# Layer norms ahead of the experts and the relative attention: the reciprocal root by a power on GpSimd, and all their coefficients made there

## The chip, the cores and the metric

The kernel runs on one NeuronCore of a Trainium2 chip. The metric is the device time of one execution in microseconds (us), lower is better. The engines are TensorE (PE; its weight loads are PEld), VectorE (DVE), ScalarE (ACT), GpSimd (POOL) and SyncE (SP, which issues DMAs). Each runs its own instruction stream, and they meet at semaphores.

## The reference

The reference is a sequence of four transformer-like layers on x of shape (8, 512, 128) in float32. Each layer is `x = x + attention(_layernorm(x))` and then `x = x + experts(_layernorm(x))`. All norms are

```python
def _layernorm(x, axis=-1, eps=1e-05):
    m = jnp.mean(x, axis=axis, keepdims=True)
    v = jnp.var(x, axis=axis, keepdims=True)
    return (x - m) / jnp.sqrt(v + eps)
```

The change concerns five of the eight norms: those ahead of the four expert blocks (top-2 GLU experts L0, switch experts L1, expert choice L2, threshold experts L3) and the one ahead of the relative-position attention of layer 3. The expert blocks also need `xn @ router` (8 or 9 columns) and a softmax over it.

## The kernel before

x stays in on-chip memory for the whole program, as 32 tiles of 128 tokens x 128 features (`chip.x`); a sequence is `TPS` = 4 tiles, and there are `B` = 8 sequences. The eight blocks run one after another. Each stage is an `nc.Block()` that gives every engine its own program and ends in a barrier over all engines.

`normalise_and_route` is one such stage and is called five times: as l0f, l1f, l2f and l3f (names of tiles carry this prefix) ahead of the experts, with a router, and as l3a ahead of the relative attention, with no router. It loops over the 8 sequences, fully unrolled, in this order for sequence i:

- VectorE makes the statistics of four tiles (`bn_stats` L513, then `bn_aggr` L517), which gives mean and variance in `mv`, 128x4 of each.
- ScalarE makes `std` = sqrt(variance + eps) (L545).
- VectorE makes `rstd` (reciprocal, L527) and `shift` = -mean x rstd (L528).
- GpSimd makes the normalised rows `xn_all` = x * rstd + shift, one instruction for a tile (L537).
- TensorE transposes the four tiles into one PSUM bank (L575), ScalarE copies the bank out (L557), and with a router TensorE multiplies the copy by it (L564), one sequence behind the transposes.
- In l0f and l1f SP stores the rows of a sequence to memory (L499) as soon as they are made.

`stats`, `mv`, `std`, `rstd` and `shift` are double-buffered. VectorE works one sequence ahead: statistics(i+1) stand before the reciprocal of sequence i. ScalarE too has the root of i+1 ahead of the copy of i. After the stage comes `route`, where VectorE takes the logits from PSUM, subtracts their maximum (L641), and ScalarE takes Exp (L715). ScalarE's functions come from tables; a function that isn't in the set loaded last has an ACT_TABLE_LOAD ahead of it, under its own line.

Two helpers matter. `Chain.link(ins)` makes an instruction count a semaphore and lets its engine wait for it, so that the next instruction starts when this one is complete. `chip.apart(eng)` puts one instruction on the engine that only counts a semaphore.

Of the kernel before, what the change touches and what calls it, by code (L numbers as in the profile page):

```python
# [7 lines left out]
ALU = mybir.AluOpType  # L8
ACT = mybir.ActivationFunctionType
# [5 lines left out]
P = 128  # L15
D = 128
B, S = 8, 512
TPS = S // P
NT = B * TPS
U = 2  # L20
LN_EPS = 1e-5
# [77 lines left out]
class Chip:  # L99


    def __init__(self, nc, ctx):
        self.nc, self.ctx = nc, ctx
        self.x = self.sb(ctx, "x", [P, NT, D])
        self.ident = self.sb(ctx, "ident", [P, P])
        self.ones = self.sb(ctx, "ones", [P, P])
        self.ln_eps = self.sb(ctx, "ln_eps", [P, 1])
        self.before = self.sb(ctx, "before", [P, P])
        self.count = self.sb(ctx, "count", [P, P])
        self.by_distance = nc.dram_tensor("by_distance", (H3, SPAN + 1), F32, kind="Internal").ap()  # L110
        self.by_place = nc.dram_tensor("by_place", (H3, P, SPAN + 1), F32, kind="Internal").ap()
        self.biases_placed = nc.alloc_semaphore(name="biases_placed")
        self.zeros = self.sb(ctx, "zeros", [P, D])
        self.token_no = self.sb(ctx, "token_no", [P, NUMBERS])
        self.apart_count = nc.alloc_semaphore(name="apart_count")
        self.counts = []
        self.banks = ctx.enter_context(nc.psum_tensor("bank", [P, 8, BANK], F32))
        self.psum = [self.banks[:, k, :] for k in range(8)]
# [9 lines left out]
    def sem(self, name):  # L128
        self.counts.append(self.nc.alloc_semaphore(name=name))
        return self.counts[-1]  # L130
# [29 lines left out]
def load_stage(chip, x_in, ident_in, before_in, count_in, token_in, rel_bias, onehot_in):  # L160


    nc = chip.nc
    inner = ExitStack()
    table, onehot, line = (chip.sb(inner, n, shape) for n, shape in (("table", [BUCKETS, H3]), ("onehot", [BUCKETS, SPAN + 1]),
                                                                      ("line", [H3, SPAN + 1])))
    table_loaded, summed, lined, line_stored = (chip.sem(n) for n in ("table_loaded", "summed", "lined", "line_stored"))
    loaded = chip.sem("x_loaded")
    with inner, nc.Block() as block:
        @block.sync  # L170
        def _(sp):
            sp.dma_start(chip.ident[:], ident_in).then_inc(loaded, 16)
            xv = x_in.rearrange("b (t p) d -> p (b t) d", p=P)
            for c in range(2):
                h = NT // 2
                sp.dma_start(chip.x[:, c * h:(c + 1) * h, :], xv[:, c * h:(c + 1) * h, :]).then_inc(loaded, 16)
            sp.dma_start(chip.before[:], before_in).then_inc(loaded, 16)
            sp.dma_start(chip.count[:], count_in.partition_broadcast(P)).then_inc(loaded, 16)
            sp.dma_start(chip.token_no[:], token_in).then_inc(loaded, 16)
            sp.wait_ge(loaded, 96)  # L180

        @block.vector
        def _(dve):
            nc.vector.memset(chip.ones[:], 1.0)
            nc.vector.memset(chip.ln_eps[:], LN_EPS)
            nc.vector.memset(chip.zeros[:], 0.0)
            for c in range(2):
                dve.wait_ge(summed, c + 1)
                dve.tensor_scalar(line[:, c * S:(c + 1) * S], chip.psum[c][0:H3, :], -1.0, None, ALU.mult).then_inc(lined, 1)

        @block.scalar
        def _(act):
            act.dma_start(table[:], rel_bias).then_inc(table_loaded, 16)
            act.dma_start(onehot[:], onehot_in).then_inc(table_loaded, 16)
            act.wait_ge(lined, 2)
            act.dma_start(chip.by_distance, line[:]).then_inc(line_stored, 16)
            act.wait_ge(line_stored, 16)

        @block.tensor
        def _(pe):  # L200
            pe.wait_ge(table_loaded, 32)
            for c in range(2):
                pe.matmul(chip.psum[c][0:H3, :], table[:], onehot[:, c * S:(c + 1) * S], start=True, stop=True).then_inc(summed, 1)
# [265 lines left out]
def normalise_and_route(chip, ctx, L, w_router, turned_out=True, rows_out=None, load_behind=None):  # L469
# [3 lines left out]
    nc = chip.nc  # L473
# [3 lines left out]
    with ExitStack() as inner:  # L477
        sb = lambda name, shape: chip.sb(inner, f"{L}r_{name}", shape)
        two = lambda name, shape: [sb(f"{name}{u}", shape) for u in range(2)]
        sem = lambda name: chip.sem(f"{L}r_{name}")  # L480
        router = sb("router", [P, NR]) if NR else None
        stats, mv = two("stats", [P, TPS, 6]), two("mv", [P, TPS, 2])
        std, rstd, shift = two("std", [P, TPS]), two("rstd", [P, TPS]), two("shift", [P, TPS])
        xnT = [xnT_all[:, i * S:(i + 1) * S] for i in range(B)] if turned_out else two("xnT", [P, S]) * (B // 2)
        loaded, stored = sem("loaded"), sem("rows_stored")
        mv_ready, std_ready, shift_ready, xn_ready = sem("mv_ready"), sem("std_ready"), sem("shift_ready"), sem("xn_ready")
        turned, xnT_ready, routed = sem("turned"), sem("xnT_ready"), sem("routed")
        dve_order = sem("dve_order")
        with nc.Block() as block:
            @block.sync  # L490
            def _(sp):
                if NR:
                    sp.dma_start(router[:], w_router).then_inc(loaded, 16)
                if rows_out is not None:
                    sp.dma_start(rows_out[0:1, :], chip.zeros[0:1, 0:D]).then_inc(stored, 16)
                    for i in range(B):
                        sp.wait_ge(xn_ready, i + 1)
                        rows = rows_out[1 + i * S:1 + (i + 1) * S, :].rearrange("(t p) d -> p t d", p=P)
                        sp.dma_start(rows, xn_all[:, i * TPS:(i + 1) * TPS, :]).then_inc(stored, 16)  # L499
                if load_behind:  # L500
                    if NR:
                        sp.wait_ge(loaded, 16)
                    load_behind(sp)
                if rows_out is not None:
                    sp.wait_ge(stored, 16 * (B + 1))

            @block.vector
            def _(dve):
                c = Chain(dve, dve_order)

                def statistics(i):
                    for t in range(TPS):
                        ins = dve.bn_stats(stats[i % 2][:, t, :], chip.x[:, i * TPS + t, :])  # L513
                    c.link(ins)
                    chip.apart(dve)
                    for t in range(TPS):
                        ins = dve.bn_aggr(mv[i % 2][:, t, :], stats[i % 2][:, t, :])  # L517
                    ins.then_inc(mv_ready, 1)

                statistics(0)  # L520
                for i in range(B):
                    if i + 1 < B:
                        statistics(i + 1)
                    dve.wait_ge(std_ready, i + 1)
                    if i >= 2:
                        dve.wait_ge(xn_ready, i - 1)
                    c.link(dve.reciprocal(rstd[i % 2][:], std[i % 2][:]))  # L527
                    dve.scalar_tensor_tensor(shift[i % 2][:], mv[i % 2][:, :, 0], -1.0, rstd[i % 2][:], ALU.mult,  # L528
                                             ALU.mult).then_inc(shift_ready, 1)

            @block.gpsimd
            def _(pool):
                for i in range(B):
                    pool.wait_ge(shift_ready, i + 1)
                    chip.apart(pool)
                    for t in range(TPS):
                        ins = pool.tensor_scalar(xn_all[:, i * TPS + t, :], chip.x[:, i * TPS + t, :], rstd[i % 2][:, t:t + 1],  # L537
                                                 shift[i % 2][:, t:t + 1], ALU.mult, ALU.add)
                    ins.then_inc(xn_ready, 1)

            @block.scalar
            def _(act):
                def deviation(i):
                    act.wait_ge(mv_ready, i + 1)
                    act.activation(std[i % 2][:], mv[i % 2][:, :, 1], ACT.Sqrt, bias=chip.ln_eps[:]).then_inc(std_ready, 1)  # L545

                deviation(0)
                for i in range(B):
                    if i + 1 < B:
                        deviation(i + 1)  # L550
                    if not (turned_out or NR):
                        continue
                    act.wait_ge(turned, i + 1)
                    if not turned_out and i >= 2:
                        act.wait_ge(routed, i - 1)
                        chip.apart(act)
                    act.copy(xnT[i][:], chip.psum[4 + i % 4][:]).then_inc(xnT_ready, 1)  # L557
# [1978 lines left out]
```

## Time and profile before

| | us |
|---|---|
| median of 3 runs | 3579.72 (3578.07 to 3584.71) |
| profiled execution, its own time | 3584.16 |
| span of that execution, first to last instruction | 3582.4 |
| TensorE matmul busy | 2932.5 |
| VectorE busy | 1922.8 |
| ScalarE busy | 1517.0 |
| GpSimd busy | 1198.6 |

The profile is of one execution. Busy times of engines overlap, so they don't add up to the span. A stretch of the program between two barriers lasts as long as its slowest chain, whatever the busy shares over the whole are.

### The profile page before, as it was taken

How to read it: one execution, taken by the hardware profiler on the slowest of the kernel's cores; microseconds unless marked ns; L12 is line 12 of the kernel's file. 1: busy time of each engine (PE TensorE's matmuls, PEld its weight loads, DVE VectorE, ACT ScalarE, POOL GpSimd, SP SyncE). 2: the span in 40 equal slices, each digit the busy share in tenths (PEclk: the TensorE clock that was granted, in tenths of full speed). 3: DMA queues.
4: the chain of work that ended last, by engine and by line, in shares of the span. 5: the costliest groups of instructions: out<-in, count | busy, mean ns of one | idle time of the engine just before them, and what ended most of it. 6: DMA issues, size and time to landing. Idle time of an engine off the chain costs nothing. (4 is left out here: it accounts for less than half of the span.)

```text
span 3582.4 us, 49632 instructions
## 1 busy us (share of the span) xinstructions
PE 2932.5 (82%) x15224; PEld 1877.2 (52%) x15224; DVE 1922.8 (54%) x4857; ACT 1517.0 (42%) x3087; POOL 1198.6 (33%) x1106
## 2 busy tenths in 40 slices
PE   7868985866845665666589599999999999799998
PEld 4658974656711221224589444444444444577776
DVE  4444446544178997997644355555555555311111
ACT  3322323121335445543233256665665666244443
POOL 0014761113715650664000245555555555200000
PEclk9977997656967996998799799999999999799999
DMA  4004661002510000001000200000000000000000
GB/s 134 0 24 135 208 174 39 0 3 86 161 34 1 1 1 0 0 0 47 1 0 0 106 1 1 0 0 0 0 0 0 0 0 1 13 6 12 6 12 23
DMA packets 75742, 110.37 MB, mean 31 GB/s; under 512 B 13442, under 2 KB 46228, under 8 KB 75588
## 3 DMA queue, kind: packets, MB, share of 16 engines
q1 hardware_dynamic: 67268, 91.70, 8.1%
q0 software_dynamic: 8192, 16.79, 2.1%
q8 instruction: 51, 0.84, 0.1%
q14 instruction: 103, 0.84, 0.1%
q10 hardware_dynamic: 128, 0.20, 0.0%
HBM read 93.91 MB, written 23.14 MB: 33 GB/s over the span
## 5 line engine op out<-in xcount | busy, mean ns | idle before, releaser
L1496 POOL TENSOR_TENSOR l3a_p<-l3a_p,l3a_rden 128x512 f32<-128x512 f32 x512 | 520.9, 1040 | 487.0 <-DVE l3a_rden L1535 484.6
L1525 DVE CUSTOM_DVE_ANT_0 l3a_p<-bank,l3a_bias 128x512 f32<-128x512 f32 x512 | 333.2, 688 | 201.5 <-PE bank L1674 195.4
L2211 POOL TENSOR_TENSOR l2a_dBu<-l2a_work,l2a_bs 128x1024 f32<-128x1024 f32 x128 | 303.3, 2373 | 327.3 <-ACT l2a_bs L2276 327.3
L1595 ACT ACTIVATE l3a_p<-l3a_p,l3a_low 128x512 f32<-128x512 f32 x512 | 365.4, 718 | 7.5 <-DVE l3a_low L1525 7.0
L1683 PEld LDWEIGHTS bank<-ident,l3a_p 128*128 128x128 f32 x2048 | 228.3, 140 | 166.8 <-issue 158.0
L2357 DVE TENSOR_TENSOR_SCAN l2a_h<-bank,l2a_dBu 128x1024 f32<-128x1024 f32 x128 | 291.9, 2281 | 5.2 <-POOL l2a_dBu L2211 5.2
L1674 PE MATMUL bank<-l3a_kT,l3a_qT 64*128 64x512 f32 x1024 | 291.2, 645 | 1.1 <-ACT l3a_kT L1586 0.7
L1601 ACT COPY l3a_pT<-bank 128x512 f32<-128x512 f32 x256 | 150.3, 587 | 324.8 <-PE bank L1683 324.4
L844 DVE SCALAR_TENSOR_TENSOR x<-bank,l3f_gates,x 128x128 f32 x256 | 85.5, 351 | 371.7 <-PE bank L872 371.7
L1683 PE MATMUL bank<-ident,l3a_p 128*128 128x128 f32 x2048 | 274.9, 277 | 3.3 <-DVE l3a_pT L1531 2.7
L2407 PE MATMUL bank<-l2a_bc,l2a_pick 128*128 128x512 bf16 x256 | 99.8, 399 | 183.4 <-DVE l2a_hc L2389 141.6
L2457 PE MATMUL bank<-l2a_hc,ident 128*128 128x512 f32 x512 | 246.5, 605 | 2.2 <-DVE l2a_xc L2363 2.2
L872 PEld LDWEIGHTS bank<-l3fe_w,l3fe_h 128*128 128x128 f32 x2048 | 233.7, 192 | 15.3 <-issue 15.3
L1692 PE MATMUL bank<-l3a_pT,l3a_v 128*64 128x512 f32 x1024 | 233.8, 598 | 0.0
L872 PE MATMUL bank<-l3fe_w,l3fe_h 128*128 128x128 f32 x2048 | 233.8, 275 | 0.0
L864 PE MATMUL bank<-l3f_xnT_all,l3fe_w 128*128 x512 | 227.3, 597 | 5.5 <-DMA l3fe_w<-in_L_ffn_W_dram 5.5
L821 ACT ACTIVATE l3fe_h<-bank,l3f_b 128x512 f32<-128x512 f32 x256 | 168.4, 689 | 142.8 <-PE bank L864 139.7
L1531 DVE COPY l3a_pT<-bank 128x512 f32<-128x512 f32 x256 | 174.4, 681 | 67.3 <-PE bank L1683 53.0
L2407 PEld LDWEIGHTS bank<-l2a_bc,l2a_pick 128*128 128x128 bf16 x256 | 25.0, 98 | 303.5 <-DVE l2a_hc L2389 225.5
L2284 ACT ACTIVATE bank<-l2a_dt,l2a_a_neg 128x511 f32<-128x511 f32 x256 | 167.0, 689 | 21.2 <-DVE l2a_h L2357 21.1
L2276 ACT COPY l2a_bs<-bank 128x512 f32<-128x512 f32 x128 | 74.9, 585 | 212.9 <-PE bank L2407 212.9
L1674 PEld LDWEIGHTS bank<-l3a_kT,l3a_qT 64*128 64x128 f32 x1024 | 78.5, 186 | 162.0 <-issue 157.2
(495 smaller groups left out, 5178.7 us busy)
## 6 DMA issues: line engine op xcount, KB each, us to landing
l0fe_wi<-in_L_ffn_in_dram SPq DMA_DIRECT2D x40, 516.0 KB, 4.7
l0fe_wo<-in_L_ffn_out_dram SPq DMA_DIRECT2D x40, 320.0 KB, 3.4
by_place<-by_distance SPq DMA_DIRECT2D x16, 512.0 KB, 11.6
l1fe_wo<-in_L_ffn_out_dram SPq DMA_DIRECT2D x24, 320.0 KB, 3.1
l3a_bias<-by_place SPq DMA_DIRECT2D x16, 448.0 KB, 12.3
l1fe_wi<-in_L_ffn_in_dram SPq DMA_DIRECT2D x24, 258.0 KB, 3.6
l0fe_answers<-l0f_y_rows SPq DMA_DIRECT2D x16, 256.0 KB, 5.0
l3fe_w<-in_L_ffn_W_dram SPq DMA_DIRECT2D x16, 256.0 KB, 3.0
```

Source lines behind the costliest of these rows:

```text
L864: bk.fill(pe.matmul(ps((n, u, j))[:], w[eh][:, j * P:(j + 1) * P], rhs, start=True, stop=True), (n, u, j))
L872: ins = pe.matmul(ps(("y", u))[:, t * D:(t + 1) * D], h[u][:, j, t * P:(t + 1) * P], w2s[eh][:, j, :], start=(j == 0), stop=(j == J - 1))
L1496: ins = pool.tensor_tensor(a, a, rden[:, t, h:h + 1].to_broadcast([P, S]), ALU.mult)
L1525: bk.drain(dve.tensor_tensor_reduce(p[u % 2][h][:, t, :], ps(job)[:], bias[:, u % HP * 2 + h, b0:b0 + S], 1.0, 3.0e38, ALU.add, ALU.min, l ...
L1531: bk.drain(dve.tensor_copy(pT[h][:, kt, :], ps(job)[:]), job)
L1595: ins = act.activation(a, a, ACT.Exp, bias=low[h][:, t:t + 1], scale=-1.0, accum_out=den[:, t, h:h + 1])
L1674: bk.fill(pe.matmul(ps(job)[:], qT[u % 2][half[h], t * P:(t + 1) * P], kT[u % 2][half[h], :], start=True, stop=True), job)
L1683: ins = pe.transpose(ps(job)[:, t * P:(t + 1) * P], p[u % 2][h][:, t, kt * P:(kt + 1) * P], chip.ident[:])
L1692: ins = pe.matmul(ps("av")[half[h], :], v[u // GP % 2][:, kt, c:c + DK3], pT[h][:, kt, :], start=(kt == 0), stop=(kt == TPS - 1))
L2211: dBu_ready.by(pool.tensor_tensor(dBu[q][:], work[u][:], bcast(bs[q][:], n_before=CH), ALU.mult))
L2357: h_ready.by(dve.tensor_tensor_scan(h[m % NH][:].rearrange("p c s -> p (c s)"), dA[m % NA].rearrange("p c s -> p (c s)"), dBu[q][:].rearra ...
L2457: ins = pe.matmul(ps(("y", u, j))[:], chip.ident[:], hc[m % NH][:, j, :], start=(n == 0), stop=(n == N - 1))
```

## The change

In `normalise_and_route` ScalarE no longer takes the root, and VectorE no longer makes reciprocal and shift; VectorE only makes the statistics. GpSimd waits for them, and makes with four instructions on 128x4: variance + eps, that to the power -0.5 (the exponent from a new constant tile `minus_half`), mean x rstd, and the product negated. Each is linked, and a counting instruction (`chip.apart`) stands ahead of each. Then come the four normalising instructions as before. Statistics of sequence i wait for the shift of sequence i-2.

```diff
--- before.py
+++ after.py
@@ -110,6 +110,7 @@
         self.by_distance = nc.dram_tensor("by_distance", (H3, SPAN + 1), F32, kind="Internal").ap()
         self.by_place = nc.dram_tensor("by_place", (H3, P, SPAN + 1), F32, kind="Internal").ap()
         self.biases_placed = nc.alloc_semaphore(name="biases_placed")
+        self.minus_half = self.sb(ctx, "minus_half", [P, 1])
         self.zeros = self.sb(ctx, "zeros", [P, D])
         self.token_no = self.sb(ctx, "token_no", [P, NUMBERS])
         self.apart_count = nc.alloc_semaphore(name="apart_count")
@@ -183,6 +184,7 @@
         def _(dve):
             nc.vector.memset(chip.ones[:], 1.0)
             nc.vector.memset(chip.ln_eps[:], LN_EPS)
+            nc.vector.memset(chip.minus_half[:], -0.5)
             nc.vector.memset(chip.zeros[:], 0.0)
             for c in range(2):
                 dve.wait_ge(summed, c + 1)
@@ -485,7 +487,7 @@
         loaded, stored = sem("loaded"), sem("rows_stored")
         mv_ready, std_ready, shift_ready, xn_ready = sem("mv_ready"), sem("std_ready"), sem("shift_ready"), sem("xn_ready")
         turned, xnT_ready, routed = sem("turned"), sem("xnT_ready"), sem("routed")
-        dve_order = sem("dve_order")
+        dve_order, pool_order = sem("dve_order"), sem("pool_order")
         with nc.Block() as block:
             @block.sync
             def _(sp):
@@ -517,22 +519,25 @@
                         ins = dve.bn_aggr(mv[i % 2][:, t, :], stats[i % 2][:, t, :])
                     ins.then_inc(mv_ready, 1)
 
-                statistics(0)
                 for i in range(B):
-                    if i + 1 < B:
-                        statistics(i + 1)
-                    dve.wait_ge(std_ready, i + 1)
                     if i >= 2:
-                        dve.wait_ge(xn_ready, i - 1)
-                    c.link(dve.reciprocal(rstd[i % 2][:], std[i % 2][:]))
-                    dve.scalar_tensor_tensor(shift[i % 2][:], mv[i % 2][:, :, 0], -1.0, rstd[i % 2][:], ALU.mult,
-                                             ALU.mult).then_inc(shift_ready, 1)
+                        dve.wait_ge(shift_ready, i - 1)
+                    statistics(i)
 
             @block.gpsimd
             def _(pool):
+                c = Chain(pool, pool_order)
                 for i in range(B):
-                    pool.wait_ge(shift_ready, i + 1)
+                    pool.wait_ge(mv_ready, i + 1)
                     chip.apart(pool)
+                    c.link(pool.tensor_scalar(std[i % 2][:], mv[i % 2][:, :, 1], LN_EPS, 0.0, ALU.add, ALU.add))
+                    chip.apart(pool)
+                    c.link(pool.tensor_tensor(rstd[i % 2][:], std[i % 2][:], chip.minus_half[:].to_broadcast([P, TPS]), ALU.pow))
+                    chip.apart(pool)
+                    c.link(pool.tensor_tensor(shift[i % 2][:], mv[i % 2][:, :, 0], rstd[i % 2][:], ALU.mult))
+                    chip.apart(pool)
+                    c.link(pool.tensor_scalar(shift[i % 2][:], shift[i % 2][:], -1.0, 0.0, ALU.mult, ALU.add))
+                    pool.sem_inc(shift_ready, 1)
                     for t in range(TPS):
                         ins = pool.tensor_scalar(xn_all[:, i * TPS + t, :], chip.x[:, i * TPS + t, :], rstd[i % 2][:, t:t + 1],
                                                  shift[i % 2][:, t:t + 1], ALU.mult, ALU.add)
@@ -540,14 +545,7 @@
 
             @block.scalar
             def _(act):
-                def deviation(i):
-                    act.wait_ge(mv_ready, i + 1)
-                    act.activation(std[i % 2][:], mv[i % 2][:, :, 1], ACT.Sqrt, bias=chip.ln_eps[:]).then_inc(std_ready, 1)
-
-                deviation(0)
                 for i in range(B):
-                    if i + 1 < B:
-                        deviation(i + 1)
                     if not (turned_out or NR):
                         continue
                     act.wait_ge(turned, i + 1)
```

GpSimd's stream at its first instructions in l0f, where `l0fr_` are the small tiles of this stage. Before:

```order
L531 UNCONDITIONAL_BRANCH
L537 ISA
L537 TENSOR_SCALAR l0f_xn_all<-x,l0fr_rstd,l0fr_shift 128x128 x32
L489 UNCONDITIONAL_BRANCH
L1039 UNCONDITIONAL_BRANCH
```

And of the change, the first two of the eight sequences (its lines stand two to four away from those of before):

```order
L527 UNCONDITIONAL_BRANCH
L533 ISA
L533 TENSOR_SCALAR l0fr_std<-l0fr_mv 128x4
L535 TENSOR_TENSOR l0fr_rstd<-l0fr_std,minus_half 128x4
L537 TENSOR_TENSOR l0fr_shift<-l0fr_mv,l0fr_rstd 128x4
L539 TENSOR_SCALAR l0fr_shift<-l0fr_shift 128x4
L542 TENSOR_SCALAR l0f_xn_all<-x,l0fr_rstd,l0fr_shift 128x128 x4
L533 TENSOR_SCALAR l0fr_std<-l0fr_mv 128x4
L535 TENSOR_TENSOR l0fr_rstd<-l0fr_std,minus_half 128x4
```

The 32 normalising instructions stood in one run, and now each four of them have four small ones ahead.

VectorE's stream at the same place, before:

```order
L513 BN_STATS l0fr_stats<-x 128x6 x4
L517 BN_AGGR l0fr_mv<-l0fr_stats 128x2 x4
L513 BN_STATS l0fr_stats<-x 128x6 x4
L517 BN_AGGR l0fr_mv<-l0fr_stats 128x2 x4
L527 RECIPROCAL l0fr_rstd<-l0fr_std 128x4
L528 SCALAR_TENSOR_TENSOR l0fr_shift<-l0fr_mv,l0fr_rstd 128x4
```

And of the change:

```order
L515 BN_STATS l0fr_stats<-x 128x6 x4
L519 BN_AGGR l0fr_mv<-l0fr_stats 128x2 x4
L515 BN_STATS l0fr_stats<-x 128x6 x4
L519 BN_AGGR l0fr_mv<-l0fr_stats 128x2 x4
L515 BN_STATS l0fr_stats<-x 128x6 x4
```

The reciprocal and the shift are gone from VectorE, here and for each further sequence. On ScalarE the 40 roots of the five stages are gone, and with them nine table loads in the compiled order: the five at L545 and the four at L715.

## Rows read from the trace of the kernel before

**Rows 1.** The page, part 1: busy us, share of the span, instructions.

```profile
PE 2932.5 (82%) x15224; PEld 1877.2 (52%) x15224; DVE 1922.8 (54%) x4857; ACT 1517.0 (42%) x3087; POOL 1198.6 (33%) x1106
```

**Rows 2.** Busy times by stretch, l0f and l3a: length, engines, granted clock, DMA.

```profile
214.00:240.60 26.60, 20.30 (x96) 19.74 (x96) 11.89 (x80) 7.71 (x17) 13.86 (x32) 0.54 0.29 80
2016.00:2037.50 21.50, 8.93 (x32) 5.73 (x32) 11.81 (x80) 7.74 (x17) 13.89 (x32) 0.50 0.57 221
```

**Rows 3.** Timeline, start of l0f: start, duration, engine, line, operation [idle before].

```profile
213.97 1.28 ACT L545 ACT_TABLE_LOAD   x1 [16.14 <-PEq L135]
214.01 0.87 DVE L513 BATCH_NORM_STATS2 l0fr_stats<-x 128x6 f32<-128x128 f32 x4 [1.08 <-PEq L135]
215.03 0.38 DVE L517 BATCH_NORM_AGGREGATE l0fr_mv<-l0fr_stats 128x2 f32<-128x6 f32 x4
...
216.60 0.14 DVE L527 RECIPROCAL l0fr_rstd<-l0fr_std 128x4 f32<-128x4 f32 x1
...
216.78 0.16 DVE L528 SCALAR_TENSOR_TENSOR l0fr_shift<-l0fr_mv,l0fr_rstd 128x4 f32<-128x4 f32 x1
...
217.23 3.45 POOL L537 TENSOR_SCALAR l0f_xn_all<-x,l0fr_rstd,l0fr_shift 128x128 f32<-128x128 f32 x8 [216.77 <-DVE l0fr_shift L528]
...
219.11 1.09 PE L575 MATMUL bank<-ident,l0f_xn_all 128*128 128x128 f32 x4 [7.71 <-POOL l0f_xn_all L537]
```

**Rows 4.** Timeline, end of l0f and start of its route stage.

```profile
230.98 1.74 POOL L537 TENSOR_SCALAR l0f_xn_all<-x,l0fr_rstd,l0fr_shift 128x128 f32<-128x128 f32 x4 [0.72 <-DVE l0fr_shift L528]
...
233.43 1.74 POOL L537 TENSOR_SCALAR l0f_xn_all<-x,l0fr_rstd,l0fr_shift 128x128 f32<-128x128 f32 x4 [0.72 <-DVE l0fr_shift L528]
...
235.71 1.09 PE L575 MATMUL bank<-ident,l0f_xn_all 128*128 128x128 f32 x4
...
240.67 1.28 ACT L715 ACT_TABLE_LOAD   x1 [3.14 <-PEq L489]
...
241.62 0.42 DVE L641 TENSOR_TENSOR l0fg_a<-l0fg_logits,l0fg_red 128x256 f32<-128x256 f32 x1
```

**Rows 5.** Timeline, start and end of l3a.

```profile
2016.21 1.28 ACT L545 ACT_TABLE_LOAD   x1 [17.23 <-PEq L1446]
2016.98 0.38 DVE L517 BATCH_NORM_AGGREGATE l3ar_mv<-l3ar_stats 128x2 f32<-128x6 f32 x4
...
2032.17 3.48 POOL L537 TENSOR_SCALAR l3a_xn_all<-x,l3ar_rstd,l3ar_shift 128x128 f32<-128x128 f32 x8 [0.89 <-DVE l3ar_shift L528]
```

**Rows 6.** Timeline, layer 1's attention: an engine ends and GpSimd starts.

```profile
568.84 0.75 DVE L1882 TENSOR_SCALAR l1a_q<-bank,l1a_bq 128x512 f32<-128x512 f32 x1 [5.76 <-PE bank L2019]
569.67 1.04 POOL L1970 TENSOR_TENSOR l1a_qsq<-l1a_q 128x512 f32<-128x512 f32 x1 [5.99 <-DVE l1a_q L1882]
...
584.30 1.06 ACT L1989 ACTIVATE l1a_fq<-l1a_fq 128x1024 f32<-128x1024 f32 x1 [14.62 <-DVEq L1916]
585.56 1.04 POOL L1975 TENSOR_SCALAR l1a_fq<-l1a_fq 128x1024 f32<-128x1024 f32 x1 [6.03 <-ACT l1a_fq L1989]
```

**Rows 7.** Groups of GpSimd instructions by shape: busy us, mean ns | idle before.

```profile
L1046 POOL DMA_INDIRECT l0fe_xs<-l0f_xn_rows,l0f_source x80 | 83.4, 1042 | 85.8 <-issue 84.9 <-DVE l0fe_y L1097 0.9
...
L1970 POOL TENSOR_TENSOR l1a_qsq<-l1a_q 128x512 f32<-128x512 f32 x8 | 8.3, 1040 | 83.8 <-DVE l1a_q L1882 83.8
...
L2202 POOL CAST l2a_pick<-l2a_part_of 128x4096 bf16<-128x4096 f32 x1 | 3.6, 3597 | 10.9 <-DMA l2a_d_par<-in_L_attn_D_param_dram 10.9
L1965 POOL TENSOR_TENSOR l1a_feat<-l1a_head_of,l1a_proj 128x256 f32<-128x256 f32 x1 | 0.6, 618 | 32.9 <-DMA l1a_bfc<-in_L_attn_bfc_dram 32.9
L1489 POOL COPY l3a_xT<-l3a_xnT_all 128x512 f32<-128x512 f32 x1 | 0.6, 609 | 2.1 <-POOLq L489 2.1
L2199 POOL MEMSET l2a_xi<- 128x6 f32 x4 | 0.2, 103 | 14.8 <-POOLq L135 14.8
```

**Rows 8.** Groups by line: the table loads of roots and of Exp.

```profile
L545 ACT ACT_TABLE_LOAD x5 | 6.4, 1283 | 65.5 <-PEq L135 48.2 <-PEq L1446 17.2
L715 ACT ACT_TABLE_LOAD x4 | 5.1, 1283 | 11.6 <-PEq L489 11.6
```

## The prediction

> **What bounds the kernel now.** I read the page first, for shares only: no engine fills the span, TensorE is busiest at 82% and GpSimd stands at 33% [rows 1]. That says nothing of this change, because the function it touches, `normalise_and_route`, is a stage of its own between barriers. So I took the five stretches in which it runs (l0f from 214.0, l1f from 799.3, l2f from 1668.7, l3a from 2016.0, l3f from 3064.7 us) and asked for each engine's busy time in them [rows 2]: two of the five stand there. Each of the four with a router lasts some 26 us and the l3a one 21.5, together 127 us, 3.6% of the span. In l0f TensorE is busy 20.3 of 26.6 us, GpSimd 13.9, VectorE 11.9, ScalarE 7.7. In l3a, which has no router matmuls, TensorE needs 8.9 and GpSimd is the busiest, 13.9 of 21.5.
>
> Then the timelines. At the start [rows 3] a sequence goes VectorE statistics, ScalarE root, VectorE reciprocal and shift, GpSimd's four normalising instructions, TensorE. The first aggregate ends at 215.41 (215.03 + 0.38), the first shift at 216.94, and GpSimd begins at 217.23. At the end [rows 4] the steady state is to be seen: GpSimd starts a sequence at 230.98 and the next at 233.43, a period of 2.45 us, of which it works 1.74 and waits 0.71. TensorE sets that period in the routed stages (1.09 for four transposes, the rest for the router). GpSimd thus has 0.71 us a sequence to give before it becomes the bound itself. In l3a [rows 5] the last GpSimd work ends at 2035.65 (2032.17 + 3.48); nothing but the chain of engines sets the pace there.
>
> **The change, part by part.** Taken away for each sequence: one ScalarE root, one VectorE reciprocal, one VectorE shift, and the two crossings between them. Added on GpSimd: add epsilon, power, product, negation, each 128x4, each linked (it waits for the one before to finish, and a count instruction stands between). Call the time from the start of the first of the four to the start of the first normalising instruction T4. GpSimd then works T4 + 1.74 for each of eight sequences. The statistics come early enough: they take 1.25 us of VectorE (0.87 and 0.38), which now does nothing else, and they may start when the shift two sequences back is done, so a whole GpSimd period lies ahead. Queued behind the four on GpSimd are the normalising instructions, and TensorE, ScalarE's copies and, in l0f and l1f, SP's row stores wait for those.
>
> A routed stage. First aggregate 215.41; GpSimd wakes 0.21 us after another engine's end when a count instruction stands ahead of its work, as 585.36 (584.30 + 1.06) to 585.56 shows for ScalarE to GpSimd, while without one it is 0.08 (569.59 to 569.67) [rows 6]. So it starts at 215.62 and ends its last sequence at 215.62 + 8 x (T4 + 1.74) = 229.54 + 8 T4. Before, that end was 235.17 (233.43 + 1.74) [rows 4]. Behind it TensorE took 0.54 us to start the last transposes since it was still routing; GpSimd-bound it starts after 0.14, as the first did (217.23 and half of the 3.45 is 218.97, to 219.11) [rows 3]: 0.40 less. The router's last matmuls stay. Change: 229.54 + 8 T4 - 235.17 - 0.40 = 8 T4 - 6.03.
>
> The l3a stage. First aggregate 2017.36, so 2017.57 + 13.92 + 8 T4 = 2031.49 + 8 T4 against 2035.65, and the tail is the same: 8 T4 - 4.16 [rows 5].
>
> All five: 4 x (8 T4 - 6.03) + 8 T4 - 4.16 = **40 T4 - 28.3**. Break-even is T4 = 0.71 us.
>
> T4 itself. Four gaps (three links and the one to the normalising) at 0.21 = 0.84; the lower bound is 0.08 each. Plain instructions [rows 7]: two-input 618 ns at 256 elements and 1040 at 512, so 1.65 ns an element and 196 ns fixed; one-input 609 ns at 512 and 3597 at 4096, so 0.83 ns and 182 fixed. At 4 elements: 0.20 for the product, 0.19 each for the add and the negation, together 0.58. Lower bound 0.10 each, a memset of 6 elements; upper bound 0.44, a quarter of the 1.74 group.
>
> The power is in no row. Below, it costs a plain two-input instruction, 0.20. Above, it must be a routine in software of many such steps on each element; twenty plain instructions would be 4.0. I take 1.0, five steps, and the nearest row with real work and little data: an indirect-DMA issue, 1.04 us [rows 7]. T4 = 0.84 + 0.58 + 1.0 = 2.42, and 40 x 2.42 - 28.3 = +68.5. The Trainium skill, "GPSIMD Engine Reference", section "Engine selection", says to keep elementwise work on VectorE, GpSimd being about half as fast at two-input work. The trace agrees in direction, since the shift that now takes two GpSimd instructions took VectorE 0.16 us [rows 3]; by a factor of two alone on VectorE's old reciprocal and shift (0.14 and 0.16) T4 would be 0.6, an estimate, and the sum -4, which lies with the second rival below.
>
> **Table loads.** The compiled order has nine fewer ScalarE table loads, five for the root and four for the Exp of `route`, 1.28 us each [rows 8]. I cost them at nothing. The root's load ran 213.97 to 215.25 while VectorE made the statistics until 215.41 [rows 3]; in l3a it ended 2017.49, 0.13 after the aggregate [rows 5], and my l3a term starts from the aggregate already. Exp's load ended 241.95, while its operand was ready at 242.04 (241.62 + 0.42) [rows 4]; the other stages with that load have the same or a later operand. If cover were missing, it would be 9 x 1.28 = 11.5 us. The Trainium skill, "ScalarE: Activation LUTs", section "Rules for kernel authors", would budget about 2.7 us for each switch of set, which is 24 us for nine, and speaks for the change; the trace has 1.28 for a load and shows it beside other work.
>
> TensorE's granted clock is 0.54 and 0.50 in these stretches [rows 2], so about its lower level of 1.2 GHz; longer pauses have little to take away, and I add nothing for it.
>
> The sum is made on the profiled execution, 3584.2 us outside and 3582.4 in the span, which is 4.4 above the median of 3579.7. The difference added to the median: 3579.7 + 68.5 = **3648**.
>
> **Rivals.**
> First, a power that goes by a long routine, or takes elements one by one. No row excludes it. Fifty plain steps are 10 us, T4 11.4, +428: 4008. Chance 0.12, for everything above T4 = 5.4.
> Second, no change: GpSimd's four pass cheaply in the 0.71 us that it waits now. It needs T4 under 0.89 (7.2 us, which is 0.2% and about what a measurement of this kernel tells). With gaps at 0.08 and instructions at 0.10 T4 is 0.32 + 0.30 + 0.20 = 0.82, +4.5: 3584. Against it: the 0.21 is seen with this very count instruction ahead. Chance 0.05.
> Third, faster: the table loads turn out to be on the path (-11.5) and T4 is small. It decides at T4 = (28.3 + 11.5 - 7.2) / 40 = 0.815. At 0.7 it gives 28 - 28.3 - 11.5 = -12: 3568. In the routed stages TensorE's 2.45 us floor stops any larger gain. Both conditions speak against their rows; chance 0.03.
> The forecast, slower by T4 between 1.34 and 5.4, has 0.80.
>
> **How the numbers follow.** Low end: gaps 0.84, three plain instructions at 0.10 and the power at 0.20, T4 1.34, +25: 3605. High end: power at 4.0, T4 = 5.42, +188.5: 3768. What lies outside is the first rival above and the other two below, 0.20. Slower 0.92, within 0.2% 0.05, faster 0.03.
>
> **What would show it.** In the profile after: GpSimd instructions of 128x4 with idle gaps near 0.21 between them; the power as the longest of the four; the last normalising group of l0f ending 8 x T4 + 14.1 us after the first aggregate; TensorE waiting for GpSimd at each sequence; no table load in these stages; the `route` stage unchanged in length. The prediction fails if the power is far from 1 us (every 0.1 is 4 us), if the links cost GpSimd much more or less than 0.21, or if something behind the stages becomes shorter with the loads gone.

## The result, and the profile after

The changed kernel takes 3650.5 us, the median of 4 runs (3646.7 to 3661.5), against 3578.9 for the kernel before in the same comparison. The ratio is 1.0207, with a 95% interval of 1.0176 to 1.0238: slower by 72 us. The prediction was 3648 in a range of 3605 to 3768. The profiled execution took 3649.3, with a span of 3647.6.

The page of the changed kernel, part 1, answers to [rows 1]. GpSimd has 67 us more and 160 more instructions, four in each of 40 sequences.

```profile
PE 2925.4 (80%) x15224; PEld 1872.7 (51%) x15224; DVE 1914.2 (52%) x4778; ACT 1494.5 (41%) x3038; POOL 1265.5 (35%) x1266
```

The busy times of l0f and l3a after the change answer to [rows 2]. Both stretches run from the first statistics to the next stage's first work. They are about 14 and 16 us longer, with GpSimd now the busiest in both, at 27.2.

```profile
212.40:253.10 40.70, 21.16 (x96) 20.13 (x96) 9.86 (x65) 4.68 (x8) 27.20 (x64) 0.52 0.18 52
2048.30:2086.00 37.70, 8.92 (x32) 5.72 (x32) 9.86 (x64) 4.68 (x8) 27.22 (x65) 0.50 0.30 122
```

The timeline at the start of l0f after the change answers to [rows 3].

```profile
213.38 0.38 DVE L519 BATCH_NORM_AGGREGATE l0fr_mv<-l0fr_stats 128x2 f32<-128x6 f32 x4
...
214.03 0.23 POOL L533 TENSOR_SCALAR l0fr_std<-l0fr_mv 128x4 f32<-128x4 f32 x1 [213.59 <-DVE l0fr_mv L519]
214.45 1.04 POOL L535 TENSOR_TENSOR l0fr_rstd<-l0fr_std,minus_half 128x4 f32<-128x4 f32 x1 [0.18 <-POOL l0fr_std L533]
...
215.67 0.20 POOL L537 TENSOR_TENSOR l0fr_shift<-l0fr_mv,l0fr_rstd 128x4 f32<-128x4 f32 x1 [0.18 <-POOL l0fr_rstd L535]
216.07 0.20 POOL L539 TENSOR_SCALAR l0fr_shift<-l0fr_shift 128x4 f32<-128x4 f32 x1 [0.20 <-POOL l0fr_shift L537]
...
216.48 1.74 POOL L542 TENSOR_SCALAR l0f_xn_all<-x,l0fr_rstd,l0fr_shift 128x128 f32<-128x128 f32 x4 [0.21 <-POOL l0fr_shift L539]
...
218.30 0.23 POOL L533 TENSOR_SCALAR l0fr_std<-l0fr_mv 128x4 f32<-128x4 f32 x1
```

T4, from the start of the add at 214.03 to the first normalising instruction at 216.48, is 2.45 us: 0.23, the power's 1.04, twice 0.20, and four gaps of 0.18, 0.18, 0.20 and 0.21. In the other sequences it is 2.43 or 2.44, except for a few pauses, the longest in l0f's fourth sequence (T4 2.80). After the group of 1.74 another 0.08 passes before the next add (218.22 to 218.30), so a sequence takes 4.26.

The end of l0f and the start of its route stage answer to [rows 4]. The last group ends at 248.38, TensorE has waited for it, and there is no table load ahead of Exp.

```profile
246.64 1.74 POOL L542 TENSOR_SCALAR l0f_xn_all<-x,l0fr_rstd,l0fr_shift 128x128 f32<-128x128 f32 x4 [0.21 <-POOL l0fr_shift L539]
...
248.44 1.11 PE L573 MATMUL bank<-ident,l0f_xn_all 128*128 128x128 f32 x4 [1.63 <-POOL l0f_xn_all L542]
...
254.46 0.42 ACT L713 ACTIVATE l0fg_ex<-l0fg_a 128x256 f32<-128x256 f32 x1 [4.18 <-DVE l0fg_a L639]
```

The whole program holds more than these stages, and its other stretches differ between executions. So I split every profiled span in two: the five stages, each from its first statistics to the first work of the next stage, and all the rest. The lengths are worked out from the first starts of the tiles concerned in the traces; each is rounded by itself, and a sum can differ from its rounded terms by 0.1. l1f and l3f end when a small DMA with the biases has landed, which VectorE waits for; in l3f that DMA took 0.6 us longer in the changed kernel, which is part of its 43.4.

| kernel | stages l0f, l1f, l2f, l3a, l3f | sum | all the rest |
|---|---|---|---|
| before | 26.7, 28.7, 26.3, 21.8, 28.7 | 132.2 | 3450.2 |
| changed | 40.7, 42.9, 40.3, 37.7, 43.4 | 205.1 | 3442.5 |

The stages account for +72.9 and the rest for -7.7, which makes the span's +65.2.

### The profile page after: what moved, and what is told of

It reads as the page before. It is cut to its first block and busy times, and to the rows that moved or that the text cites. A ratio compares the mean times of both kernels' runs of the same rounds, so it can differ in the third digit from the quotient of the medians.

```text
span 3647.6 us, 49794 instructions
## 1 busy us (share of the span) xinstructions
PE 2925.4 (80%) x15224; PEld 1872.7 (51%) x15224; DVE 1914.2 (52%) x4778; ACT 1494.5 (41%) x3038; POOL 1265.5 (35%) x1266
## 6 DMA issues: line engine op xcount, KB each, us to landing
l3a_bias<-by_place SPq DMA_DIRECT2D x16, 448.0 KB, 11.5
```

## The experiments

The first four ran beside 15 runs of the kernel before with a median of 3580.0, e5 to e8 beside 16 with 3581.3. Their stage sums can be set beside 132.2 and 205.1.

### e1_product: a product in place of the power

```diff
-c.link(pool.tensor_tensor(rstd[i % 2][:], std[i % 2][:], chip.minus_half[:].to_broadcast([P, TPS]), ALU.pow))
+c.link(pool.tensor_tensor(rstd[i % 2][:], std[i % 2][:], chip.minus_half[:].to_broadcast([P, TPS]), ALU.mult))
```

> The changed kernel with the power's operation replaced by a plain product of the same two tiles, so the root isn't computed and the rows are scaled wrongly. My theory: the power costs its profile duration on GpSimd's own chain, so each falls from 1.03 to about 0.20 us, T4 from 2.44 to 1.61 us, and the program by 40 x 0.83 = 33 us to about 3617. Rival (what costs is the number of linked instructions, and the power's long duration overlaps the crossings): less than 10 us, so 3640 or more.

Measured: 3625.7 (3621.0 to 3626.7), ratio 1.0120 (1.0105 to 1.0136); stages 34.0, 36.0, 33.6, 31.0, 36.7, sum 171.4. The group in l0f:

```profile
L535 POOL TENSOR_TENSOR l0fr_rstd<-l0fr_std,minus_half 128x4 f32<-128x4 f32 x8 | 1.6, 198 | 1.8 <-POOL l0fr_std L533 1.8
```

The stages fell by 33.7, where 33 was expected. The power is paid in full. The median fell by 25 only; the rest of the program took 3452.7 in this profile against 3442.5 in the changed kernel's.

### e2_no_counts: three counting instructions fewer

```diff
 c.link(pool.tensor_scalar(std[i % 2][:], ...))
-chip.apart(pool)
 c.link(pool.tensor_tensor(rstd[i % 2][:], ..., ALU.pow))
-chip.apart(pool)
 c.link(pool.tensor_tensor(shift[i % 2][:], ...))
-chip.apart(pool)
 c.link(pool.tensor_scalar(shift[i % 2][:], ...))
```

> The changed kernel without the counting instruction ahead of the power, the product and the negation (the one ahead of the add stays). My theory, from the two crossings of the profile before: the gap of 0.18 to 0.21 us is 0.08 of waking and 0.12 of the counting instruction, so three gaps fall to about 0.08, T4 by 0.36, and the program by 40 x 0.36 = 14 us to about 3636. Rival (the gap is what one GpSimd instruction takes to complete and be seen by the next, and the counting instruction is done meanwhile): under 3 us, so 3648 to 3653, with gaps still near 0.2.

Measured: 3641.5 (3636.8 to 3648.3), ratio 1.0164 (1.0148 to 1.0179); stages 37.9, 40.3, 37.8, 35.2, 40.9, sum 192.2. Its timeline, one sequence of l0f:

```profile
222.63 0.23 POOL L533 TENSOR_SCALAR l0fr_std<-l0fr_mv 128x4 f32<-128x4 f32 x1
222.95 1.03 POOL L534 TENSOR_TENSOR l0fr_rstd<-l0fr_std,minus_half 128x4 f32<-128x4 f32 x1
224.06 0.20 POOL L535 TENSOR_TENSOR l0fr_shift<-l0fr_mv,l0fr_rstd 128x4 f32<-128x4 f32 x1
224.35 0.20 POOL L536 TENSOR_SCALAR l0fr_shift<-l0fr_shift 128x4 f32<-128x4 f32 x1
...
224.76 1.74 POOL L539 TENSOR_SCALAR l0f_xn_all<-x,l0fr_rstd,l0fr_shift 128x128 f32<-128x128 f32 x4 [0.21 <-POOL l0fr_shift L536]
```

The three gaps are now 0.09, 0.08 and 0.09, and the fourth, which still has a counting instruction in it, is 0.21. T4 is 2.13. So a link of GpSimd to itself costs 0.09 and the counting instruction 0.09 to 0.12; the stages fell by 12.9 (14 expected). The median fell by 9.0, with 3454.4 in the rest.

### e3_no_shift: (x - mean) * rstd

```diff
-chip.apart(pool)
-c.link(pool.tensor_tensor(shift[i % 2][:], mv[i % 2][:, :, 0], rstd[i % 2][:], ALU.mult))
-chip.apart(pool)
-c.link(pool.tensor_scalar(shift[i % 2][:], shift[i % 2][:], -1.0, 0.0, ALU.mult, ALU.add))
-pool.sem_inc(shift_ready, 1)
...
-ins = pool.tensor_scalar(xn_all[...], chip.x[...], rstd[i % 2][:, t:t + 1], shift[i % 2][:, t:t + 1], ALU.mult, ALU.add)
+ins = pool.tensor_scalar(xn_all[...], chip.x[...], mv[i % 2][:, t, 0:1], rstd[i % 2][:, t:t + 1], ALU.subtract, ALU.mult)
```

VectorE's wait for the shift two sequences back becomes one for the rows.

> The changed kernel with no shift: GpSimd normalises by (x - mean) * rstd, so the product and the negation and their two links are gone. The result is the same function. My theory: T4 falls by two instructions of 0.20 and two gaps of 0.2, 0.79 us, and the program by 32 us to about 3619; still 40 us slower than before. Rival (the normalising instructions wait for something else, such as VectorE's statistics, and use the slack): less than 10 us.

Measured: 3669.4 (3667.0 to 3671.2), ratio 1.0244 (1.0229 to 1.0260); stages 43.6, 46.1, 43.8, 40.9, 46.6, sum 221.1. Both expectations missed: it is slower than the changed kernel. One sequence and the group:

```profile
224.92 0.24 POOL L533 TENSOR_SCALAR l0fr_std<-l0fr_mv 128x4 f32<-128x4 f32 x1
...
225.34 1.03 POOL L535 TENSOR_TENSOR l0fr_rstd<-l0fr_std,minus_half 128x4 f32<-128x4 f32 x1 [0.18 <-POOL l0fr_std L533]
...
226.47 3.13 POOL L537 TENSOR_SCALAR l0f_xn_all<-x,l0fr_mv,l0fr_rstd 128x128 f32<-128x128 f32 x4
```

T4 did fall, to 1.55 (224.92 to 226.47), 0.89 less. But the four normalising instructions take 3.13 us where they took 1.74, which is 1.39 more. The 0.08 us ahead of the next add is gone as well. Either the operations or the operands of the normalising instructions are dearer; e5 and e6 were made to tell which.

### e4_no_loads: the kernel before without table loads

```diff
-act.activation(std[i % 2][:], mv[i % 2][:, :, 1], ACT.Sqrt, bias=chip.ln_eps[:]).then_inc(std_ready, 1)
+act.activation(std[i % 2][:], mv[i % 2][:, :, 1], ACT.Identity, bias=chip.ln_eps[:]).then_inc(std_ready, 1)
```

> The kernel before with ScalarE's root replaced by Identity with the same bias, which needs no table load of its own, so the root is left out and the rows are scaled wrongly. The nine table loads go, and nothing else changes. My theory: they lie beside other work, so the time is that of before within 0.1%, 3576 to 3582. Rival: they are on the path of their stages, -11.5 us, about 3568. At most 0.2 us of it should be seen in each stage's length.

Measured: 3581.8 (11 runs, 3574.6 to 3584.9), ratio 0.9999 (0.9990 to 1.0008); stages 26.7, 28.7, 26.3, 21.8, 28.7, all five as before. All nine loads are gone from its trace. The four ahead of Exp lay behind the stages' ends as counted here, but from the first work on the logits to the start of Exp it takes 1.37 us in l0f, l1f and l2f, and 1.41 in l3f, in this kernel, in the one before and in the changed one alike. The loads were covered; the rival's -11.5 us would be a ratio of 0.9968.

### e5_mult_subtract and e6_columns: what makes normalising slow

```diff
 # e5, from the changed kernel
-chip.apart(pool)
-c.link(pool.tensor_scalar(shift[i % 2][:], shift[i % 2][:], -1.0, 0.0, ALU.mult, ALU.add))
...
-ins = pool.tensor_scalar(..., rstd[i % 2][:, t:t + 1], shift[i % 2][:, t:t + 1], ALU.mult, ALU.add)
+ins = pool.tensor_scalar(..., rstd[i % 2][:, t:t + 1], shift[i % 2][:, t:t + 1], ALU.mult, ALU.subtract)
 # e6, from e3
-ins = pool.tensor_scalar(..., mv[i % 2][:, t, 0:1], rstd[i % 2][:, t:t + 1], ALU.subtract, ALU.mult)
+ins = pool.tensor_scalar(..., mv[i % 2][:, t, 0:1], rstd[i % 2][:, t:t + 1], ALU.mult, ALU.add)
```

> The changed kernel without the negation: shift is mean * rstd, and GpSimd normalises by x * rstd - shift, which is the same function. e3_no_shift normalised by (x - mean) * rstd and its 128x128 instructions took 0.795 us where they took 0.448. Theory A (multiply then add has a short path on GpSimd and any other pair of operations goes the long way): 0.79 here too, so T4 falls by 0.4 and the four instructions grow by 1.37, +0.97 a sequence, 39 us over the changed kernel, about 3689. Theory B (only subtract as the first operation is slow): 0.45 here, -0.4 a sequence, -16 us, about 3634.

> The kernel of e3_no_shift with multiply and add in place of subtract and multiply, on the same operands (mean column and rstd column), so the rows are wrong. Theory A or B (the operations are the cause): 0.45 us an instruction, and the program falls to that of e3 less 40 x 1.37 = 55 us, about 3614, which is the changed kernel less the two instructions and two gaps. Theory C (the mean's column, every second element of its tile, is slow to fetch): 0.79 and 3669 as in e3.

Measured: e5 3697.6 (3693.1 to 3703.5), ratio 1.0320 (1.0304 to 1.0336), stage sum 240.6, 35.5 more than the changed kernel's (39 expected by theory A). e6 3617.8 (3615.6 to 3620.2), ratio 1.0101 (1.0086 to 1.0116), stage sum 165.1, 56.0 less than e3 (55 expected). The l0f groups, e5's first:

```profile
L540 POOL TENSOR_SCALAR l0f_xn_all<-x,l0fr_rstd,l0fr_shift 128x128 f32<-128x128 f32 x32 | 25.0, 794 | 1.7 <-POOL l0fr_shift L537 1.7
```

```profile
L537 POOL TENSOR_SCALAR l0f_xn_all<-x,l0fr_mv,l0fr_rstd 128x128 f32<-128x128 f32 x32 | 13.9, 448 | 0.8
```

Multiply-add on the mean's column is fast, and multiply-subtract on the old columns is slow. The operations decide and the operands don't. Of the three pairs tried, (multiply, add) takes 0.448 us and (subtract, multiply) and (multiply, subtract) take 0.794. Both slow pairs hold a subtraction, so whether it is the subtraction that costs or any pair other than (multiply, add) isn't shown.

### e7_pairs: coefficients of two sequences at once

```diff
-stats, mv = two("stats", [P, TPS, 6]), two("mv", [P, TPS, 2])
-std, rstd, shift = two("std", [P, TPS]), two("rstd", [P, TPS]), two("shift", [P, TPS])
+stats, mv = two("stats", [P, 2 * TPS, 6]), two("mv", [P, 2 * TPS, 2])
+std, rstd, shift = two("std", [P, 2 * TPS]), two("rstd", [P, 2 * TPS]), two("shift", [P, 2 * TPS])
...
-for i in range(B):
+for i in range(B // 2):
     pool.wait_ge(mv_ready, i + 1)
```

The loops over tiles of VectorE and GpSimd go over eight, and `xn_ready` is counted after each four.

> The changed kernel with the coefficients of two sequences made at once: four instructions on 128x8 ahead of eight normalising ones, and the statistics in pairs as well; the same function. Theory A (the power is paid by the element): 1.03 becomes 0.20 + 2 x 0.83 = 1.86 us, T4 of a pair 3.3; each stage saves 4 x (2.51 - 0.83) and starts 1.25 us later, so -5.5 a stage, -27 in all, about 3623. Theory B (paid by the instruction): the power stays 1.03, T4 of a pair 2.45, -8.8 a stage, -44 in all, about 3606.

Measured: 3617.5 (3614.1 to 3629.4), ratio 1.0107 (1.0086 to 1.0127); stages 34.7, 37.0, 34.5, 31.1, 36.9, sum 174.2. The group in l0f:

```profile
L535 POOL TENSOR_TENSOR l0fr_rstd<-l0fr_std,minus_half 128x8 f32<-128x8 f32 x4 | 6.6, 1660 | 0.7 <-POOL l0fr_std L533 0.7
```

Neither theory holds as put. The power takes 1.03 us for 4 elements a partition and 1.66 for 8: from the two, 0.40 fixed and 0.16 an element, where a plain product stays at 0.20 for both. T4 of a pair is 3.08 in the timeline, so a stage saves 4 x (2 x 2.44 - 3.08) = 7.2 and four times 0.08, which is 7.5. It loses 1.0 at the start, where statistics of eight tiles come first (2.43 us where it was 1.40). A routed stage loses 0.8 more at the end, where TensorE begins the last transposes 0.82 us behind GpSimd and not 0.06. That makes 6.5 for l3a and 5.7 for a routed stage, 29.3 in all; the stages fell by 30.8, of which the earlier landing of the biases in l3f is 0.6.

### e8_roots_ahead, e9_ahead_l3a, e10_ahead_routed: the old way with roots earlier

```diff
-stats, mv = two("stats", [P, TPS, 6]), two("mv", [P, TPS, 2])
-std, rstd, shift = two("std", [P, TPS]), two("rstd", [P, TPS]), two("shift", [P, TPS])
+stats, mv = eight("stats", [P, TPS, 6]), eight("mv", [P, TPS, 2])
+std, rstd, shift = eight("std", [P, TPS]), eight("rstd", [P, TPS]), eight("shift", [P, TPS])
...
-deviation(0)
+for i in range(4):
+    deviation(i)
 for i in range(B):
-    if i + 1 < B:
-        deviation(i + 1)
+    if 4 <= i + 3 < B:
+        deviation(i + 3)
```

VectorE's wait for the rows of two sequences back goes too, since no buffer is used twice. e9 and e10 have this in l3a alone and in the routed stages alone, with roots ahead by three at most.

> The kernel before (root on ScalarE, reciprocal and shift on VectorE) with eight buffers of the small tiles and ScalarE's roots up to three sequences ahead of its copies, so that no root stands behind a copy that waits for TensorE. The same function. My theory: in l3a GpSimd then works without pause, and its last group ends at about 2033 where it ended at 2035.65, -2.5 us; in the four routed stages TensorE's 2.45 us a sequence stays and only its first pauses go, -1 each; in all -6, about 3574. Rival (the order of roots is covered): 3580, stage lengths unchanged within 0.3 us.

> The kernel before with e8's eight buffers and roots ahead in the l3a stage alone. e8 made the l3a stage 2.8 us shorter, while the relative attention behind it took 6.6 us more (VectorE's copies of its output, first to last, 985.1 us where every other run has 978.2 to 978.8). Theory A (the attention's loop depends on how the l3a stage leaves the engines or on what it leaves in the code and the memory map): the loop takes 985 us here too, and the time is 3584. Theory B (it comes from the l3f or the other stages' code): the loop takes 978 and the time is 3577. If the loop takes 978 in both this and the next kernel, the 6.6 us are a spread from build to build that one profile can't place.

> The same in the four routed stages alone, with l3a as before. TensorE's 2.45 us a sequence stays, so each of these stages keeps its length within 0.3 us. Theory A: the attention's loop takes 978 us and the time is 3580. Theory B: it takes 985 and the time is 3587.

| kernel | stages | sum | the rest | ratio to before (95%) |
|---|---|---|---|---|
| e8 | 26.5, 28.5, 26.1, 19.0, 28.8 | 128.9 | 3454.3 | 1.0010 (1.0002 to 1.0019) |
| e9 | 26.7, 28.8, 26.3, 19.1, 28.7 | 129.6 | 3492.4 | 0.9998 (0.9984 to 1.0013) |
| e10 | 26.5, 28.6, 26.1, 22.0, 28.7 | 131.8 | 3500.5 | 1.0002 (0.9990 to 1.0015) |

e9 and e10 ran on another chip, on which the kernel before took 3632.5; only their ratios and stages are compared. In e8's l3a, GpSimd works through its 32 instructions without a pause:

```profile
2016.21 13.74 POOL L536 TENSOR_SCALAR l3a_xn_all<-x,l3ar_rstd,l3ar_shift 128x128 f32<-128x128 f32 x32 [333.35 <-DVE l3ar_shift L527]
```

The l3a stage is 2.8 us shorter in e8 (2.5 expected) and 2.6 in e9. The routed stages stay within 0.3 us of their lengths, bound by TensorE; e8's expectation of -1 each missed. In total nothing is won: e8's median is 3585.3 where 3574 was expected. In e8 the stretch between l3a and l3f grew from 1027.0 to 1033.7; in e9 and e10 it is 1027.0 and 1027.6. So it is neither of the two edits by itself, and what lengthened it in e8 stays open. The 2.6 us of e9 are 0.07%, less than its interval can show. No version tried beats the kernel before.

## Why the prediction was right, point by point

**GpSimd becomes the bound of all five stages.** Right. TensorE waits for it at each sequence. l3a grew more (16.0) than the routed stages (14.0 to 14.7): before, GpSimd took 16.5 us from its first to its last normalising instruction there, and 17.8 to 18.0 in the routed stages, which TensorE's 2.45 us a sequence held back. With the small instructions between them it now takes 34.0 to 34.4 in all five.

**T4 = 2.42.** It measured 2.44. The gaps, predicted at 0.21 each from the crossings of [rows 6], were 0.18, 0.18, 0.20 and 0.21. Plain instructions, from the two lines through [rows 7], were predicted at 0.20 and 0.19 and took 0.20, 0.20 and, for the add, 0.23. The power was the guess of the sum, 1.0 between 0.2 and 4.0; it took 1.03. That the value was so near is luck: five plain steps, or the likeness to an indirect-DMA issue, is no reason for it. e1 shows that what the power takes is paid in full (33.7 for 33). e2 shows the split of a gap into waking and counting instruction, as [rows 6] had it.

**40 T4 - 28.3.** With 2.44 it gives 69.3; the stages grew by 72.9. The missing 3.6 are mostly the 0.08 us between a normalising group and the next add, which I took as nothing: 0.08 x 7 x 5 = 2.8, or 3.0 unrounded. e3, e5 and e6, with two or three small instructions in place of four, don't have this gap, and its cause stays open. The pauses in T4 add 0.3, and another 0.3 comes of taking l0f's times before for all four routed stages. The first waking, 0.21 in the prediction, was 0.28 us in l0f and 0.19 to 0.21 in the other four. The end of a routed stage came out right only in sum. TensorE began the last transposes 0.06 us behind GpSimd, not 0.14, and the router's last matmuls didn't stay as they were. From GpSimd's end to the stage's end it took 0.83, 0.33 and 0.46 us less in l0f, l1f and l2f and 0.04 more in l3f, 1.6 in all, where I had four times 0.40.

**Table loads cost nothing.** Shown by e4, with all five stages unchanged to 0.1 us and Exp no earlier. The rule of the Trainium skill, "ScalarE: Activation LUTs", section "Rules for kernel authors", to budget for each switch of set, priced a thing that this kernel did beside its statistics.

**The rest of the program.** I forecast no change there. In the profile it was 7.7 us shorter, within what profiles of these kernels differ by: over the changed kernel and e1 to e8 it goes from 3442.5 to 3460.9. It isn't the loads either, since e1 and e2, which have none of the nine, took 3452.7 and 3454.4. So the agreement of 3648 with 3650.5 is closer than the method can claim; the stage sum is the fair comparison, 68.5 against 72.9.

**TensorE's clock adds nothing.** Not quite. The stretch behind l3f is 488.9 us before and 492.4 after. All of the difference has come about when VectorE adds the first output of the experts to x, 39.5 us into it before and 43.1 after; from there on both take the same 449.4 us to within 0.1. The granted clock ahead of that, first the kernel before, then the changed one, in 10 us from 10 us after the route stage's first work:

```profile
3103.50:3113.50 10.00, 10.00 (x76) 9.45 (x75) 7.63 (x12) 0.00 (x0) 0.00 (x0) 0.84 0.00 0
```

```profile
3165.10:3175.10 10.00, 10.00 (x62) 9.13 (x61) 6.43 (x10) 0.00 (x0) 0.00 (x0) 0.67 0.00 0
```

Before, the granted clock was 1.00 (2.4 GHz) from 3103.7 to 3110.5, then 0.50 (1.2 GHz), and 1.00 again from 3124.2. After, it was 0.99 from 3166.3 to 3169.7 only, which is half as long, then 0.50, and 1.00 from 3190.2, which is 35.1 us into the stretch where it was 30.7. So 76 matmul records fit in the 10 us before, and 62 after. Of the 64 gate matmuls there (L739, after the change L737), 48 ran at the high clock before and 22 after, with a median of 0.270 us each, and the others at the low one, with 0.416. So the 3.6 us arise where the clock differs. What made it differ is less clear. Ahead of it TensorE was busy 20.3 us of l3f's 28.7 before, and paused for each sequence after. e6 and e7 have pauses too, but in them the clock stood at 2.4 GHz as long as before, and the stretch is 488.7 and 488.8; in e1 it stood so as briefly as in the changed kernel, with 492.5. So the pauses alone don't decide, and what does stays open.

**The rivals.** No change would have needed T4 under 0.89, faster under 0.815 with the loads on the path; neither condition came near. The long routine, at 50 plain steps, is excluded by 1.03 for the power. The factor of two for GpSimd against VectorE of the Trainium skill, "GPSIMD Engine Reference", section "Engine selection", an estimate of T4 = 0.6, left out the links: of 2.44 us the gaps alone are 0.77, and the power 1.03.

## What to carry to other kernels

Price work that moves to an engine by what that engine already has to do in a turn: here 0.71 us of slack against 2.44 us of added chain, of which a third was gaps between linked instructions on a handful of elements. The nine table loads cost nothing here, since ScalarE wasn't late with them; look at what a load runs beside before moving a function for its sake. And when a function is rewritten algebraically, check the engine's price for the new pair of operations: dropping two of GpSimd's instructions made the stage slower, since the rewritten normalisation took 0.79 us instead of 0.45.

## What the hardware showed that I had not expected

- GpSimd's 128x128 tensor-scalar with two column operands took 0.448 us with (multiply, add) and 0.794 with (subtract, multiply) or (multiply, subtract), on the same columns (e3, e5, e6).
- GpSimd's power took 1.03 us on 128x4 and 1.66 on 128x8, each time nearly the same (the groups' means are 1.023 to 1.031 and 1.657 to 1.661); the product took 0.20 on both.
- A counting instruction between two linked GpSimd instructions cost 0.09 to 0.12 us, about as much as the link itself, 0.09 (e2).
- The kernel before took 3580 us on one chip and 3632 on another, where it has no profile of its own. In e9 and e10, profiled on the second, nearly all of the difference lies between l0f and l2f: against the profile of the kernel before, 20.5 and 24.0 us in the two stretches in e9, 26.5 and 23.4 in e10.
